# State-space chunk loop: causal mask moved from TensorE products to an absolute value on ScalarE and one VectorE product

## What is computed

```python
dt = jax.nn.softplus(dt + dt_bias)
A = -jnp.exp(A_log)
dA = jnp.exp(dt * A)
def step(state, inputs):
    dA_t, dt_t, x_t, B_t, C_t = inputs
    state = dA_t[:, :, None, None] * state + (dt_t[:, :, None] * x_t)[..., None] * B_t[:, None, None, :]
    y_t = jnp.einsum('bhpn,bn->bhp', state, C_t)
    return (state, y_t)
```

## Time and profile before

| what | value |
|---|---|
| median of 3 runs | 1664.44 us (1663.12 to 1665.12) |
| the profiled execution, its own time | 1660.48 us |
| its span, first to last instruction | 1658.7 us |
| outside the span | 1.8 us |
| mean granted TensorE clock | 0.891 of 2.4 GHz |
| busy: PE, DVE, ACT, POOL | 80%, 66%, 40%, 25% of the span |
| line 1050, the masking products | 128 instructions |
| line 852, the exponentials | 128 instructions, 597 ns each |
| ACT table loads in the profile | 1283 ns each, none inside the chunk loop |

### The profile page before, as it was taken

How to read it: one execution, slowest core, us unless ns; L and a number is a source line. 1 busy time by engine, 2 the same in 40 slices (tenths; PEclk the granted TensorE clock), 3 DMA queues, 4 the chain that set the end, 5 groups by cost and what they waited for, 6 DMA issues and landing times.

```text
span 1658.7 us, 34449 instructions
## 1 busy us (share of the span) xinstructions
PE 1331.2 (80%) x12846; PEld 915.7 (55%) x12847; DVE 1091.9 (66%) x1669; ACT 670.3 (40%) x1011; POOL 415.0 (25%) x390
## 2 busy tenths in 40 slices
PE   3734799998358999984559999974899999999991
PEld 2214566765246676642235555561777777776770
DVE  3576888887568888877875455555556775576333
ACT  3236454453545445422350111132446664466330
POOL 0121344444223454340224242315000000000003
PEclk9757899999679999997869989865999999999996
DMA  8042000000300000013120000024536552445004
GB/s 297 23 148 93 2 2 1 1 1 4 132 32 3 1 1 1 1 52 153 40 98 1 0 0 0 0 87 180 219 127 227 216 214 110 169 163 186 25 25 158
DMA packets 34029, 132.30 MB, mean 80 GB/s; under 512 B 6665, under 2 KB 8457, under 8 KB 24017
## 3 DMA queue, kind: packets, MB, share of 16 engines
q1 hardware_dynamic: 25808, 103.19, 17.1%
q0 software_dynamic: 8160, 28.32, 4.9%
HBM read 108.82 MB, written 22.68 MB: 79 GB/s over the span
## 4 chain that ended last, share of the span: by engine, by line
PE 48%; issue 17%; DVE 15%; POOL 11%; DMA 4%; ACT 4%; POOLq 0%; DVEq 0%; SPq 0%; ACTq 0%
PE banks L2102 14%; PE banks L2123 13%; PE banks L1644 6%; PE banks L1721 3%; POOL mb_quad L942 2%; POOL mb_ysq L906 2%; PE banks L1697 2%; DVE mb_ca L592 2%; POOL mb_quad L934 1%; POOL mb_ring L929 1%; POOL mb_ysq L892 1%; POOL xs_table L2135 1%; PE banks L1002 1%; DVE mb_S L679 1%; PE banks L340 1%
## 5 line engine op out<-in xcount | busy, mean ns | idle before, releaser
L2102 PE MATMUL banks<-eb_x_hi,eb_w_hi 128*128 128x128 f16 x1344 | 228.4, 220 | 2.0 <-DVE eb_x_lo L2002 2.0
L2102 PE MATMUL banks<-eb_x_lo,eb_w_hi 128*128 128x128 f16 x1344 | 228.4, 220 | 0.0
L2102 PE MATMUL banks<-eb_x_hi,eb_w_lo 128*128 128x128 f16 x1344 | 228.3, 220 | 0.0
L978 PE MATMUL banks<-mb_u_hi,mb_wi_hi 128*128 (+3 forms) x1152 | 199.8, 220 | 22.0 <-ACT mb_ca L805 22.0
L978 PE MATMUL banks<-mb_u_hi,mb_wi_lo 128*128 (+3 forms) x1152 | 199.4, 220 | 0.0
L978 PE MATMUL banks<-mb_u_lo,mb_wi_hi 128*128 (+3 forms) x1152 | 199.4, 220 | 0.0
L2102 PEld LDWEIGHTS banks<-eb_x_hi,eb_w_hi 128*128 128x128 f16 x1344 | 132.3, 98 | 4.8 <-issue 2.4
L2102 PEld LDWEIGHTS banks<-eb_x_lo,eb_w_hi 128*128 128x128 f16 x1344 | 132.3, 98 | 2.4
L2102 PEld LDWEIGHTS banks<-eb_x_hi,eb_w_lo 128*128 128x128 f16 x1344 | 132.3, 98 | 0.0
L978 PEld LDWEIGHTS banks<-mb_u_hi,mb_wi_hi 128*128 128x128 f16 (+1 forms) x1152 | 112.8, 98 | 34.8 <-issue 27.1
L2123 PE MATMUL banks<-eb_w_lo,eb_h_hi 128*128 x336 | 128.1, 381 | 0.0
(11 more groups left out here) (431 smaller groups left out, 3240.6 us busy)
## 6 DMA issues: line engine op xcount, KB each, us to landing
eb_raw<-e_w SPq DMA_DIRECT2D x36, 1024.0 KB, 5.0
eb_un<-e_w SPq DMA_DIRECT2D x28, 1024.0 KB, 7.4
mb_ring<-m_in_w SPq DMA_DIRECT2D x8, 1072.0 KB, 5.5
xs_table<-zero POOLq DMA_DIRECT2D x1, 6400.0 KB, 20.7
eb_xg<-xs_table POOLq DMA_DIRECT2D x23, 256.0 KB, 2.9
ys_table<-eb_y POOLq DMA_DIRECT2D x21, 256.0 KB, 6.6
ab_raw<-a_in_w SPq DMA_DIRECT2D x4, 1154.0 KB, 11.9
mb_ring<-m_out_w SPq DMA_DIRECT2D x4, 1024.0 KB, 5.2
```

The source lines that it names most:

```text
L978: x = e.matmul(ps[0:width, bank, n * P:(n + 1) * P], a[:, k, f:f + width], b[:, k, ds(i * P, P)], start=(k == 0 and m == 0), stop=(k == KD ...
L2102: o = e.matmul(ps[:, j, c * P:(c + 1) * P], a[:, side, k, f * P:(f + 1) * P], b[:, k, :], start=(k == 0 and m == 0), stop=(k == KD - 1 and ...
```

## The change

The difference of cum is negative or zero where s <= t and positive or zero above the diagonal. The new kernel takes exp(-|difference|), which is the same number below the diagonal and a finite one above it, and puts the zeros into B.C instead, once per chunk.

- TensorE no longer issues line 1050; each group is one product, and it waits for `distant` (the absolute value has left the bank) where it waited for `exped`.
- ScalarE takes for two groups the absolute value, bank to slot, and then for the same two groups the exponential with scale -1, slot to slot in place. Each exponential waits for its own `distant`.
- VectorE multiplies B.C in bank 2 (128 columns) by the triangle constant into the next 128 columns of the same bank, waits for that itself (`gm_done`), and the 8 products of a chunk read this copy.
- Two constants and their two loads go.

```diff
-        for dst, name in ((sel, "c_sel3"), (ident16, "c_ident16"), (never, "c_never")):
-            e.dma_start(dst[:], ins[name]).then_inc(fixed_in, 16)
+        e.dma_start(sel[:], ins["c_sel3"]).then_inc(fixed_in, 16)
...
                 e.wait_ge(bt_done, g + 1)
+                e.tensor_tensor(ps[:, 2, 2 * P:3 * P], ps[:, 2, P:2 * P], core.tri[:], ALU.mult).then_inc(gm_done, 1)
+                e.wait_ge(gm_done, g + 1)
                 for k in range(MB_EG):
                     e.wait_ge(exped, g * MB_EG + k + 1)
...
-                                    ps[:, 2, P:2 * P].unsqueeze(1).to_broadcast([P, MB_HG, P]), ALU.mult)\
+                                    ps[:, 2, 2 * P:3 * P].unsqueeze(1).to_broadcast([P, MB_HG, P]), ALU.mult)\
...
-                for k in range(MB_EG):
+                def distance(k):
                     e.wait_ge(diff, MB_EG * g + k + 1)
                     if k >= MB_ER:
                         e.wait_ge(m_done, MB_EG * g + k - MB_ER + 1)
-                    e.activation(E[:, 512 * (k % MB_ER):512 * (k % MB_ER + 1)], ps[:, 3 + k % 2, :], ACT.Exp).then_inc(exped, 1)
+                    e.activation(E[:, 512 * (k % MB_ER):512 * (k % MB_ER + 1)], ps[:, 3 + k % 2, :], ACT.Abs).then_inc(distant, 1)
+
+                for k in range(MB_EG):
+                    if k % MB_ER == 0:
+                        for n in range(MB_ER):
+                            distance(k + n)
+                    e.wait_ge(distant, MB_EG * g + k + 1)
+                    slot = E[:, 512 * (k % MB_ER):512 * (k % MB_ER + 1)]
+                    e.activation(slot, slot, ACT.Exp, scale=-1.0).then_inc(exped, 1)
                     if not is_first and k == 1:
                         upper_y(g - 1)
...
                     if k >= 2:
-                        e.wait_ge(exped, MB_EG * g + k - 1)
-                    e.matmul(ps[:, 3 + k % 2, :], ident16[:], never[:].unsqueeze(1).to_broadcast([P, MB_HG, P]), start=True, stop=False)
-                    e.matmul(ps[:, 3 + k % 2, :], cum[:, ds(i * P, P)], pairs[:, 512 * k:512 * k + 512], start=False, stop=True)\
+                        e.wait_ge(distant, MB_EG * g + k - 1)
+                    e.matmul(ps[:, 3 + k % 2, :], cum[:, ds(i * P, P)], pairs[:, 512 * k:512 * k + 512], start=True, stop=True)\
                         .then_inc(diff, 1)
```

More of the change, by code:

```diff
@@ L362 @@
 MB_K = MB_CR + MB_SPLIT
-MB_NEVER = -60000.0
 MB_LNW, MB_LNB, MB_CVW, MB_CVB, MB_BCW, MB_BCB, MB_DCOL, MB_RMSW, MB_DTB, MB_ALOG = 0, 4, 8, 40, 48, 56, 58, 66, 74, 106
@@ L397, in stage_mamba @@
     sel = sb("sel", [MB_CR, JD, P], F16)
-    ident16, never = sb("ident16", [P, P], F16), sb("never", [P, P], F16)
     cum_rows = nc.dram_tensor("cum_rows", [MB_CR, TOK], F16).ap()
@@ L438, in stage_mamba @@
     xtr, x_scaled, g_mm, bt_done = (sem(n) for n in ("xtr", "x_scaled", "g_mm", "bt_done"))
-    diff, exped, m_done = sem("diff"), sem("exped"), sem("m_done")
+    diff, distant, exped, m_done, gm_done = (sem(n) for n in ("diff", "distant", "exped", "m_done", "gm_done"))
     ecum_mm, ec_done, inter_mm, yi_done, yid_done, dx_done = (
@@ L1024, in pe @@
             e.wait_ge(w_lo, (l + 1) * MB_PIECES)
-            e.wait_ge(fixed_in, 4 * 16)
+            e.wait_ge(fixed_in, 2 * 16)
             e.wait_ge(ones_set, 1)
@@ L2254, in shape_constants @@
     c["c_pairs"] = np.tile(np.repeat(-np.eye(H2, dtype=np.float16), P, 1), (MB_SPLIT, 1))
-    c["c_ident16"] = np.eye(P, dtype=np.float16)
-    c["c_never"] = (MB_NEVER * c["c_after"]).astype(np.float16)
     c["c_selT"] = (np.arange(H2)[None, None, :] == 4 * j + k[:, None, None] // 32).astype(np.float32)
```

## The result

| | before | after |
|---|---|---|
| median of the runs | 1664.24 us (1663.12 to 1665.12, 4 runs) | 1708.91 us (1702.62 to 1713.45, 4 runs) |
| the profiled execution, its span | 1660.48, 1658.7 us | 1711.4, 1709.6 us |
| mean granted TensorE clock | 0.891 | 0.870 |
| a middle chunk at full clock | 31.62 us | 32.80 us |

The kernel became slower: ratio 1.027, 95% interval 1.024 to 1.030, 44.7 us by the medians. The forecast was 1699.3, which is 9.6 us too low; its range, up to 1711, holds the result.

The account below looks back on a forecast made before the run. ScalarE's queue, with 2.78 us idle, was taken to bound the group stretch. 14.0 + 1.2 + 2.6 + 15.6 + 1.5 = 34.9 us on the profiled 1660.5 gave 1695.4, plus 3.9 to the median: 1699.3; range 1678 to 1711.

Parts of the forecast that it names:

- What bounds the kernel: Middle chunk's group stretch (11.88 us): it ends when ScalarE has come through its queue, which has only 2.78 us idle.
- The middle chunk, 1.17 us: Group stretch of a middle chunk: ScalarE's added absolute values lengthen it from 11.88 to 13.05 us, 14.0 over 12 chunks.
- TensorE's saving, nothing: Middle chunks: the eight removed masking products of 0.22 us come out of TensorE's waiting time, so gain nothing.
- VectorE's product, nothing: Added triangle product on bank 2: 0.3 us (0 to 0.5), covered by the y rounding, so it costs nothing.
- First and last chunks: Outer chunks of the loops: first chunks 0.6 us longer each, 1.2; last chunks 1.3 each, 2.6.
- The clock, 15.6 us: Emptier TensorE in the group stretch drops to half clock in nearly all middle chunks: 1.3 x 12 = 15.6 us.
- the first place: TensorE's wait ahead of group 4's product in a middle chunk; the forecast's clock falls slow projections of groups 4 to 7.
- The second place: TensorE's wait ahead of the B and C projection, forecast 2.7 us instead of 1.32; a fall there costs 1.5.
- rival 2: Two clock falls a chunk, the added one behind the wait ahead of the B and C projection: 1715 us, chance 0.08.
- Rival 1: No clock falls in the chunk loops: only 17.8 us added, 1682.2 us, chance 0.22.
- Rivals 3 and 4: ScalarE operations follow closer: faster, 1647 us at 0.37 spacing (chance 0.07), or the same, 1664 near 0.44 (chance 0.05).
- Rival 5: ScalarE's absolute value needs another function table, each load costing 1.28 us; given no chance.

Follow-up runs that it names:

- ScalarE's part alone: Kernel before, masks kept, with a second ScalarE operation per group (absolute value slot to slot after the exponential) in the change's pair order: 1707.93 us, ratio 1.027.
- the run with three slots: Changed kernel with three slots for the exponentials instead of two, same ScalarE order, one small buffer shared: 1707.69 us, ratio 1.025.
- the run with the first place filled: Changed kernel with 8 unread TensorE products after group 3 of each middle chunk, ahead of group 4: 1703.82 us, ratio 1.023.
- the unread products: Changed kernel with 8 TensorE products nobody reads after group 3 and 8 after the last x projection of each middle chunk: 1686.05 us, ratio 1.014.

## Why the prediction was right, and where not

**What bounds the kernel: right in the main.** ScalarE's 2.78 us of slack in the stretch decided, and not its busy share of 45%. ScalarE's part alone costs 2.05 us a chunk, and of its slack 0.29 us are left as an idle row. But the prediction had TensorE's chain 0.24 us ahead of need at group 7, and it is not ahead: the run with three slots shows that at the end of the stretch both bind.

**The middle chunk, 1.17 us: right.** 1.18 measured, with ScalarE's two times quoted above within 0.03 us; since TensorE's product comes 0.28 us later than forecast (9.00 for 8.72), part of that closeness is luck. The spacing of the absolute value is 0.49 (1.09 less 0.60) and of the exponential out of SBUF 0.52, against 0.49 and 0.53 taken; the bounds of 0.04 on each were not needed.

**TensorE's saving, nothing: right in the sum, wrong as a statement of its worth.** The forecast of 13.05 us was worked out with the masks gone already. Against keeping them, their removal is worth 0.87 us a chunk at full clock. In the kernel before, together with VectorE's product, it gives 0.25, and there the clock took more back.

**VectorE's product, nothing: right here.** Alone it costs 0.42 us a chunk, as the sentence on its cover warned, and not 0.3: the wait for itself, which the upper bound of 0.5 held, counts too.

**First and last chunks:** the first chunks took 1.6 more for 1.2. The path from the first absolute value to the eviction is 9.71 us in layer 0, as worked out (9.7), and that chunk, with a fall that it did not have before, grew by 1.0 for 0.6. In layer 1 the first chunk begins at half clock and the path is 11.04; that it grew by 0.54 for 0.6, with other falls than before, is luck. The output projection of the last chunks starts 7.87 us after the first product (forecast 7.7). First product to row sum grew by 2.2 and 2.7, together 5.0 for 4.1; in both layers the fall there is twice as long as the one in layer 0 before.

**The clock, 15.6 us: the mechanism was right, the size was not. This is the term that failed**, "I expect falls in nearly all chunks ... 1.3 x 12 = 15.6". The middle chunks lost 24.8. The step counted one fall a chunk, at the first place. Measured were eight falls there, eight at the second, a third one in one chunk and a double length in another. Over these 18 lengths the price is 1.4 each (24.8 / 18), close to the 1.3: the price was right and the count was wrong. The second place had been written down as rival 2, with a chance of 0.08 and a price of 1.5. Its place, behind the gap ahead of the B and C projection (2.35 us where I gave 2.7), and its price (1.4 to 1.65 in the run with the first place filled) are what the runs show. Its chance was too low: the prediction gave the second gap a length and a price, but no row on how likely a fall behind it was. Rival 2's full form, two falls in every chunk, did not come either: 16 of 24 did. The measured 1708.9 lies between the forecast and its 1715. It lies inside the range because the high end, 1711, took in part of rival 2 and 7 us for a wider spacing on ScalarE, which did not come; that margin stood in for the missing falls, so the hit is in part luck.

**Rival 1** (no falls, 1682.2) is what the unread products made: 1686.05, with one middle chunk and the first chunks at a lower clock still. **Rivals 3 and 4** wanted the operations closer than 0.49; none is. **Rival 5**: no table load stands in the chunk loops.

The Trainium skill ("TensorE: Matmul & The Clock Gate", Part 1: The HAM clock gate) describes half rate as the state of an idle engine. Read strictly, the trace disagrees again: 1.36 busy us in 3.70, with six products, were followed by a clock of 0.51. Nor did the load ahead decide alone, as the prediction had reasoned, since 1.38 in 3.70 was followed by 1.00.

## What to carry over

An engine's slack is the idle time in its queue between the two events that bound the stage, not the rest of its busy share; before adding work to an engine, see whether work of the *next* stage that stands in its tail can use that slack (here half an eviction, 21.6 us). When a change thins TensorE's work, list every place that becomes emptier and price a clock fall at each; what is removed as unneeded may be what kept the clock up. If a stretch must have gaps, a run with unread products in one gap at a time tells what each costs.

## What was not expected of the hardware

- Identical code with equal load ahead of it (1.36 and 1.38 busy us in 3.70) is followed by a clock of 0.51 in one chunk and 1.00 in another. Chunks of 32.8, 33.9, 35.4 and 37.0 us stand side by side, and the four runs of the changed kernel spread over 11 us, where those of before beside them spread over 2 (4 to 9 in the later sets of six to nine). What decides which chunk has a fall is not shown.
- Sixteen unread 512-column products a chunk made the kernel 22.9 us faster. With products in one place only, the falls at the other became regular, and 17.8 or 21.6 us of those 22.9 were lost again.
- The absolute value of a 128x512 tile, which the trace of before did not hold, takes 0.60 us and 0.49 us to the next start, the same as the exponential; the prediction took this over, with a bound of 0.04 either side, and it held.
